# Graph network on one core: the 8-head layer's turned one-hots go to GpSimd, its rescaling to ScalarE, and each summation layer's first adjacency group gets memory of its own

## What is computed

```python
def gat_edge(x, W, a_src, a_dst, edge_W, edge_b, bias, edge_attr, src, dst):      # 8 heads
    h = (x @ W.T).reshape(n, 8, 32)
    alpha = einsum('ehd,hd->eh', h[src], a_src) + einsum('ehd,hd->eh', h[dst], a_dst)
    enc = relu(edge_attr @ edge_W.T + edge_b).reshape(-1, 8, 32)
    alpha = leaky_relu(alpha + sum(enc * h[dst], -1), 0.2)
    ex = exp(alpha - segment_max(alpha, dst)[dst])
    out = segment_sum(h[src] * (ex / segment_sum(ex, dst)[dst])[..., None], dst)
    return out + bias
def sage(x):                                   # three times, relu between
    mean = segment_sum(x[src], dst) / max(deg, 1)
    return mean @ Wl.T + bl + x @ Wr.T
def gcn(x):                                    # self-loops added, symmetric normalisation
    return relu(norm_d * segment_sum((norm_s * (x @ W))[src], dst) + b)
```

## Time and profile before

| | before |
|---|---|
| median of 3 runs | 3315.35 us (3314.17 to 3328.64) |
| profiled execution, its own time | 3314.46 us |
| its span, first to last instruction | 3312.6 us |
| TensorE busy / VectorE / ScalarE / GpSimd | 2700.5 / 1819.1 / 1223.2 / 1470.2 us |
| layer 0, from GpSimd's gathers of group 4 to those of group 51 and their period | 306.5 to 907.5 us |
| summation layers, first to last matmul | 1031.2 to 2008 us, with a node stage of some 50 us between two of them |

### The profile page before, as it was taken

How to read it: one execution, slowest core, us unless ns; L and a number is a source line. 1 busy time by engine, 2 the same in 40 slices (tenths; PEclk the granted TensorE clock), 3 DMA queues, 4 the chain that set the end, 5 groups by cost and what they waited for, 6 DMA issues and landing times.

```text
span 3312.6 us, 50756 instructions
## 1 busy us (share of the span) xinstructions
PE 2700.5 (82%) x12657; PEld 1721.4 (52%) x12658; DVE 1819.1 (55%) x4880; ACT 1223.2 (37%) x3147; POOL 1470.2 (44%) x1469
## 2 busy tenths in 40 slices
PE   6997998989989999999997997466677747766765
PEld 4774555555655545545555555344455535544543
DVE  6996999999962010000005005466666547666665
ACT  2774555555521001001001002644444454444445
POOL 5402766666613004004005001777777347777760
PEclk8998999999979999999998999777777868788785
DMA  7456877777712322322321332455545235555541
GB/s 230 130 125 171 225 214 207 206 219 209 211 21 82 100 63 77 98 70 67 101 77 62 104 98 63 131 140 136 136 136 143 77 109 136 140 141 139 138 114 40
DMA packets 310915, 421.17 MB, mean 127 GB/s; under 512 B 56707, under 2 KB 245047, under 8 KB 310367
## 3 DMA queue, kind: packets, MB, share of 16 engines
q1 hardware_dynamic: 235679, 231.06, 24.2%
q0 software_dynamic: 60544, 173.03, 19.6%
q10 hardware_dynamic: 14400, 13.93, 1.4%
HBM read 378.03 MB, written 39.84 MB: 126 GB/s over the span
## 4 chain that ended last, share of the span: by engine, by line
PE 43%; POOL 17%; issue 15%; DVE 14%; DMA 4%; ACT 4%; DVEq 2%; SPq 1%; ACTq 1%; POOLq 0%
PE ps L762 24%; POOL rows L2155 17%; PE ps L1002 3%; PE ps L633 3%; DMA rows<-table,src_idx 2%; DVE norm L1344 2%; PE ps L982 2%; PE ps L721 2%; PE ps L612 2%; ACT norm L1173 1%; PE ps L922 1%; DVE al L1350 1%; PE ps L819 1%; DVE segmax L1386 1%; PE ps L932 1%
## 5 line engine op out<-in xcount | busy, mean ns | idle before, releaser
L2155 POOL DMA_INDIRECT rows<-table,src_idx x1248 | 1251.7, 1003 | 511.6 <-issue 367.1
L762 PE MATMUL ps<-rows,rT 128*128 128x448 f16 x2800 | 765.4, 355 | 20.3 <-DMA rows<-adjacency 12.8
L762 PE MATMUL ps<-rows,spread 128*128 128x448 f16 x1400 | 497.1, 355 | 0.0
L762 PEld LDWEIGHTS ps<-rows,rT 128*128 128x128 bf16 x2800 | 275.4, 98 | 281.2 <-issue 29.2
L1556 DVE TENSOR_TENSOR rows<-ps,norm 128x896 f32<-128x896 f32 x21 | 22.9, 1092 | 636.7 <-PE ps L762 636.7
L2109 POOL CAST rT<-rows 128x1024 bf16<-128x1024 f32 (+1 forms) x28 | 30.1, 1074 | 727.6 <-ACT rows L1288 508.9
L819 PE MATMUL ps<-rows,spread 128*128 128x260 f32 x832 | 278.8, 503 | 67.6 <-DVE rows L1667 67.2
L819 PE MATMUL ps<-rows,w_roots 128*128 128x260 f32 x832 | 270.0, 490 | 37.7 <-DVE rows L1667 37.6
L819 PEld LDWEIGHTS ps<-rows,spread 128*128 128x128 f32 x832 | 207.2, 257 | 122.8 <-DVE rows L1667 71.5
L1667 DVE TENSOR_TENSOR rows<-rows,ps 128x1024 f32<-128x1024 f32 x208 | 249.0, 1197 | 30.2 <-issue 25.6
L612 PE MATMUL ps<-rT,spread 128*128 128x264 f32 x832 | 247.1, 422 | 4.1 <-DMA rT<-table 2.1
(11 more groups left out here) (270 smaller groups left out, 4302.5 us busy)
## 6 DMA issues: line engine op xcount, KB each, us to landing
rows<-adjacency SPq DMA_DIRECT2D x140, 560.0 KB, 4.0
rT<-table SPq DMA_DIRECT2D x316, 136.0 KB
spread<-in_tiles SPq DMA_DIRECT2D x104, 256.0 KB, 4.4
rows<-table,src_idx POOLq DMA_INDIRECT x1248
rT<-table ACTq DMA_DIRECT2D x100, 136.0 KB
w_table<-in_tiles SPq DMA_DIRECT2D x52, 256.0 KB
adjacency<-rT SPq DMA_DIRECT2D x4, 2800.0 KB, 13.7
adjacency<-acc SPq DMA_DIRECT2D x3, 2800.0 KB, 13.6
```

What stands on the lines that cost most here:

```text
L762: ins = mm(chunk_ps[c % 2][:, f, :], xp[k][:, t, f * P:(f + 1) * P], ring[q][:, i, :], start=t == 0 and k == 0, stop=t == ROWS - 1 and k = ...
L2155: pool.indirect_dma_start(src_rows(l, par)[:, k, :], None, tables[l][:, :], bass.IndirectOffsetOnAxis(ap=src_idx[:, g * T + k:g * T + k + ...
```

## The change

Three edits that do not depend on each other:

1. The turned one-hots of groups 4 to 51 are made by GpSimd, between the group's fourth and fifth gather, behind the wait for `h_ready` that stood there and a new wait for `high_landed`; VectorE makes those of groups 0 to 3 ahead of its loop.
2. `rescale_node` runs on ScalarE, between the fourth `encoded` and `node_sums_out`: three ACTIVATEs (two columns of `acc`, one of `den`) with a per-partition scale, and a register load for the node's number, in place of two VectorE instructions and their register load.
3. `ring[0]` moves to words 6656 to 7776 of `rows`, behind the node stage's scratch, and the other four to words 0 to 4480. The first piece of a layer waits for the node stage's first row in place of its last; the other four wait for the last row and no longer for the parts. TensorE takes the groups of chunks 0 and 1 in the order (0,0) to (0,3), (1,0) to (1,2), (0,4), (1,3), (1,4), and `USED_AT` gives the waits that follow from it. `weighed` keeps one buffer.

```diff
-        ring = [rows[:, q * PIECE:(q + 1) * PIECE].bitcast(F16).rearrange("p (h c) -> p h c", h=HQ) for q in range(NQ)]
+        ring_at = [8704 - FC * CC - 32 - PIECE] + [q * PIECE for q in range(NQ - 1)]
+        ring = [rows[:, ring_at[q]:ring_at[q] + PIECE].bitcast(F16).rearrange("p (h c) -> p h c", h=HQ) for q in range(NQ)]
...
-        weighed = [rows[:, 8704 - (b + 1) * FC * CC:8704 - b * FC * CC].rearrange("p (f n) -> p f n", f=FC) for b in range(2)]
-        more_weighed = weighed[0][:, :, 0:SPAN]
+        weighed = rows[:, 8704 - FC * CC:8704].rearrange("p (f n) -> p f n", f=FC)
+        more_weighed = weighed[:, :, 0:SPAN]
...
+        SUM_ORDER = [(0, q) for q in range(NQ - 1)] + [(1, q) for q in range(NQ - 2)] + [(0, NQ - 1), (1, NQ - 2), (1, NQ - 1)]
+        SUM_ORDER += [(c, q) for c in range(2, PIECES) for q in range(NQ)]
+        USED_AT = {of: i + 1 for i, of in enumerate(SUM_ORDER)}
+
...
-            for c in range(PIECES):
-                if c > 1:
-                    pe.wait_ge(window_added, PIECES * (l - 1) + c - 1)
-                for q in range(NQ):
+            for c, q in SUM_ORDER:
+                if c > 1 and q == 0:
+                    pe.wait_ge(window_added, PIECES * (l - 1) + c - 1)
...
+            def rescale_node(g, par):
+
+                node = act.value_load(base[0:1, bass.ds(g, 1)], min_val=0, max_val=N)
+                if isinstance(g, int) and g == 0:
+                    act.wait_ge(acc_cleared, 1)
+                act.wait_ge(resc_copied, g + 1)
+                act.wait_ge(added, g + 1)
+                for f in range(FC):
+                    col = acc[:, f, bass.ds(node, 1)]
+                    nc.scalar.activation(col, col, ACT.Copy, scale=resc_f[par][:, f:f + 1])
+                dcol = den[0:H, bass.ds(node, 1)]
+                nc.scalar.activation(dcol, dcol, ACT.Copy, scale=resc_f[par][0:H, FC:FC + 1]).then_inc(rescaled, 1)
+
...
+                rescale_node(g, j % 2)
...
-            def rescale_node(g, par):
-
-                node = V.value_load(base[0:1, bass.ds(g, 1)], min_val=0, max_val=N)
-                if isinstance(g, int) and g == 0:
-                    dve.wait_ge(acc_cleared, 1)
-                dve.wait_ge(resc_copied, g + 1)
-                dve.wait_ge(added, g + 1)
-                col = acc[:, :, bass.ds(node, 1)]
-                V.tensor_tensor(col, col, resc_f[par][:, 0:FC].unsqueeze(2), ALU.mult)
-                dcol = den[0:H, bass.ds(node, 1)]
-                V.tensor_tensor(dcol, dcol, resc_f[par][0:H, FC:FC + 1], ALU.mult).then_inc(rescaled, 1)
-
...
-                of_n, of_x = next_group(j, h, 1), next_group(j, h, 3)
+                of_n = next_group(j, h, 1)
...
-                if m is not None and not is_last(m):
-                    turned_hots(m + 1, *of_x)
...
-                rescale_node(g, j % 2)
-                if m is not None:
...
+            turned_hots(3, 3, 0)
...
-                dve.wait_ge(piece_used, NQ * (before + c + 1))
+                dve.wait_ge(piece_used, NQ * before + USED_AT[c, NQ - 1])
...
-                    V.tensor_tensor(weighed[c % 2], summed, of_nodes, ALU.mult).then_inc(window_weighed, 1)
+                    V.tensor_tensor(weighed, summed, of_nodes, ALU.mult).then_inc(window_weighed, 1)
...
-                    V.tensor_tensor(acc[:, :, of], acc[:, :, of], weighed[c % 2], ALU.add).then_inc(window_added, 1)
+                    V.tensor_tensor(acc[:, :, of], acc[:, :, of], weighed, ALU.add).then_inc(window_added, 1)
...
-                            sp.wait_ge(piece_used, NQ * PIECES * (l - 1) + at - NQ + 1)
-                        elif q < 3:
-                            sp.wait_ge(row_ready, ROWS * (l + 1))
+                            sp.wait_ge(piece_used, NQ * PIECES * (l - 1) + USED_AT[c - 1, q])
+                        elif q == 0:
+                            sp.wait_ge(row_ready, ROWS * l + 1)
...
-                            sp.wait_ge(parts_ready, NCH * l)
+                            sp.wait_ge(row_ready, ROWS * (l + 1))
...
+                            wait_alone(pool, high_landed[g % 2], 16 * (g // 2 + 1))
+                            nc.gpsimd.tensor_scalar(edge_turned[:, g % 2, :, :].rearrange("p t e -> p (t e)"), high_row[:, g % 2, :],
+                                                    rank[:, 0:1], None, ALU.is_equal).then_inc(edge_turned_ready, 1)
```

More of the change, by code:

```diff
@@ L746, in sum_pe @@
             pe.wait_ge(row_out, ROWS * (l + 1))
-            for c in range(PIECES):
-                if c > 1:
+            for c, q in SUM_ORDER:
+                if c > 1 and q == 0:
                     pe.wait_ge(window_added, PIECES * (l - 1) + c - 1)
-                for q in range(NQ):
[L752 to L764, removed]
+                if c == 0:
+                    pe.wait_ge(parts_ready, NCH * (l - 1) + 1 + -(-(HQ * (q + 1) - 1) // 4))
+                if l not in MEAN_LAYERS and q in loop_rows(c):
+                    pe.wait_ge(loops_added, loops_upto(c, q))
+                else:
+                    pe.wait_ge(piece_landed[q], 16 * (PIECES * (l - 1) + c + 1))
+                for i in range(HQ):
+                    t = HQ * q + i
+                    for f in range(FC):
+                        for k in range(PARTS):
+                            ins = mm(chunk_ps[c % 2][:, f, :], xp[k][:, t, f * P:(f + 1) * P], ring[q][:, i, :],
+                                     start=t == 0 and k == 0, stop=t == ROWS - 1 and k == PARTS - 1)
+                ins.then_inc(piece_used, 1)
             def window(w):
@@ L1989, in load_adjacency @@
                         if c > 0:
-                            sp.wait_ge(piece_used, NQ * PIECES * (l - 1) + at - NQ + 1)
-                        elif q < 3:
+                            sp.wait_ge(piece_used, NQ * PIECES * (l - 1) + USED_AT[c - 1, q])
+                        elif q == 0:
+                            sp.wait_ge(row_ready, ROWS * l + 1)
+                        else:
                             sp.wait_ge(row_ready, ROWS * (l + 1))
-                        else:
-                            sp.wait_ge(parts_ready, NCH * l)
                         sp.dma_start(ring[q], adjacency[:, q * HQ:(q + 1) * HQ, c * CC:(c + 1) * CC]).then_inc(piece_landed[q], 16)
```

## The result

The changed kernel takes 3346.16 us (median of 6 runs, 3344.89 to 3349.09) against 3314.76 us before (6 runs): ratio 1.0093, 95% interval 1.0072 to 1.0114. It is slower by about 31 us; 3284 us was forecast. The profiled execution has a span of 3345.7 us against 3312.6, 33.1 us more.

| us | before | after | difference |
|---|---|---|---|
| start to the first messages of layer 0 | 290.0 | 292.2 | +2.1 |
| first to last group's messages | 636.1 | 699.2 | +63.1 |
| from there to the first summation matmul | 105.1 | 100.2 | -4.9 |
| summation layers | 976.9 | 955.1 | -21.8 |
| 4-head layers, code untouched | 1304.5 | 1299.0 | -5.5 |

A forecast was written before the change was run, and what follows sets the result against it. Layer 0 was bound by VectorE, its 12.00 us step falling to the TensorE-ScalarE ring's 11.73: 13 us less. Summation layers gave 10.2 + 3.2 + 4.8, 18 less; together 31, so 3284 us, range 3258 to 3325.

The forecast's parts named there:

- the cast's 1.04 us: Layer 0, GpSimd: price taken for the 1024-column comparison, plus 0.1 us start, giving 11.9 us a group.
- the ring of TensorE and ScalarE: Layer 0: mutual waits of both engines, 10.98 us a step, 11.73 with the ACTIVATEs; ends last, 13 us less.
- GpSimd becomes the bound: Rival, layer 0: comparison costing as the two-input form makes groups of 13.62 us, kernel 3350 us; chance 0.10.
- the forecast's condition: Layer 0, GpSimd: comparison of about 1.05 us, so GpSimd's group stays at 11.9 us; forecast 31 us less.
- The ACTIVATEs: Layer 0, ScalarE: three instructions for rescaling add 0.75 us to the ring, bounds 0.51 and 1.17.
- the sum had 13: Layer 0: 0.27 us less per step over 48 groups, 13 us of the forecast's gain.
- over 2 us to spare: Layer 0: GpSimd's one-hots come over 2 us before TensorE's spread needs them.
- the rule: Layer 0: VectorE's two-input and GpSimd's SBUF-reading instructions exclude each other throughout; VectorE loses at most 1.04 us a step.
- the three first waits: Summation layers: TensorE's waits for the first piece in three layers, 12.8 us, shrink to 0.85 each; 10.2 us less.
- the fourth: Fourth summation layer: of TensorE's 7.5 us wait, 4.3 stay behind VectorE's self-loop adds and 3.2 go.
- the clock, of which half was taken: Summation layers' starts: shorter waits may keep TensorE's clock up; bounds 0 and 9.6 us, 4.8 taken.
- Order and late pieces: Summation layers: new group order costs nothing; later pieces stay hidden, the fifth possibly 0 to 2 us a layer.

The follow-up runs named there:

- the copy run: Changed kernel with GpSimd copying the same tiles in place of comparing them (spread features of groups 4 to 51 wrong): 3263.11 us, ratio 0.9839.
- the half run: Changed kernel with GpSimd comparing four of the eight tiles and VectorE the other four at the old place: 3292.74 us, ratio 0.9939.
- the filling matmuls: Three small unread matmuls per layer 0 step in TensorE's pauses; added to edits 2 and 3: 3270.65 us, again 3272.96; added to the changed kernel: 3348.99.

## Why the prediction was wrong

- **GpSimd's comparison: the step that failed.** The prediction took the cast's 1.04 us because the comparison has one tensor input, and set the two-input form's 2.17 us as the upper bound. It costs 2.86 us: the number of tensor inputs was the wrong likeness, and the bound wasn't one. With it GpSimd's queue, and not the ring of TensorE and ScalarE, ends last, and layer 0 is 63 us longer instead of 13 shorter. No row of the trace before showed a TENSOR_SCALAR on GpSimd. The Trainium skill ("GPSIMD Engine Reference", Engine selection) calls one-input work on GpSimd roughly line-rate; the copies' 1.04 us for 1024 columns agree, TENSOR_SCALAR's 2.77 to 2.86 us do not.
- **The rival that held.** "GpSimd becomes the bound" had the mechanism and the point from which it decides (1.77 us for what is put in), and its 3350 us lies 4 us from the result, but by luck, since errors cancel: its group of 13.62 us was 13.90 us (comparison, start and the waits that are left 3.05 us instead of 2.27, gathers longer by 0.1 instead of 0.6), and the summation layers gave 27 us instead of 18. It had a chance of 0.10, and the range stopped at 3325 us, short of it. The run with the copy shows the forecast's condition: at 1.05 us the kernel gains 53 us, more than the 31 of the forecast.
- **ScalarE and the ring.** The ACTIVATEs cost 0.56 us against 0.75 taken (0.51 to 1.17). With edits 2 and 3 alone the step is VectorE's 11.61 us, and in the copy run it goes down to 11.2: the ring's 10.98 us without them was too long by at least 0.3 us. Layer 0 is 28 us shorter there, where the sum had 13. What the prediction did not have is the clock: with edits 2 and 3 it falls in 13 of 41 steps, in the kernel before in 6, behind pauses of TensorE that both have. Such a fall makes a step of 11.6 us 0.8 to 2.6 us longer, one of the kernel before 0.3 to 0.6, and the matmuls in the pauses give 11 to 14 us of layer 0 back. Why it falls more often stays open.
- **One-hots in time.** TensorE's spread, to which the prediction gave over 2 us to spare, waits for GpSimd's one-hots in ten groups, 9.0 us in all and 2.7 us at most.
- **VectorE and the port.** Its two-input instructions are held up, as feared, but not for as long as the rule read. VectorE's timeline in the changed kernel, and GpSimd's comparison beside it:

```profile
743.75 2.20 DVE L1404 SCALAR_TENSOR_TENSOR segmax<-pens,carry_of,segmax 64x128 f32<-64x128 f32 x2
...
757.67 0.71 DVE L1404 SCALAR_TENSOR_TENSOR segmax<-pens,carry_of,segmax 64x128 f32<-64x128 f32 x2
```

```profile
744.68 2.86 POOL L2159 TENSOR_SCALAR spread<-spread,rank 128x1024 f32<-128x1024 bf16 x1
```

  The first pair ends at 745.95, 1.27 us into the comparison; the second stands free. In 27 of the 47 groups such a pair ends 1.26 to 1.28 us behind the comparison's start, though in 26 of them its second instruction had begun 0.20 to 0.64 us ahead of that start. Of the Trainium skill's rule ("SBUF — State Buffer", SBUF: two separate sides), that the loser waits for the whole instruction, the trace shows the waiting, but of 2.86 us only the first 1.27. That it costs nothing here, since GpSimd's queue sets the step anyway, is argued and not tried.
- **Summation layers.** Right in kind, too small in size: the three first waits gave 10.6 us (12.8 - 2.2; 10.2 taken), the fourth 5.4 (7.5 - 2.1; 3.2 taken, mainly since the four self-loop adds took 1.44 us instead of 3.27), and the clock, of which half was taken (4.8), gave all: the 1050 matmuls of the four layers take 198.4 us each from the first start to the last instead of 201.1, 200.1, 201.4 and 200.5, 9.3 us together before rounding. Order and late pieces cost nothing, as said.

## What to carry to other kernels

A price taken from the nearest row holds only for the same kind of instruction: before work moves to GpSimd, time the very form it will have there (a few instructions behind a layer do, run twice, since another engine can hold one of them up), because a queue that is straight code with 1.8 us of room turns an error of 1.8 us into the bound of a whole layer. Where such an unmeasured price decides, its rival needs a chance that matches, and the range must reach it. When a step is shortened, look at TensorE's granted clock step by step: here its falls behind small pauses took back half or more of what layer 0 had gained (11 of 23 us, 14 of 21), and a few spare matmuls in the pauses returned that to the layer, though not all of it to the kernel.

## What the runs showed that was not expected

- On GpSimd, TENSOR_SCALAR over 1024 columns takes 2.77 to 2.86 us when nothing holds it up, with a constant or a per-partition operand, is_equal or mult, bf16 or f32; a copy or cast 1.04, a two-input subtraction 2.34.
- VectorE's two-input instructions are held up until 1.27 us after the start of such a TENSOR_SCALAR of 2.86 us, and until 1.20 us after that of a cast of 1.05 us (the copy run). The longer of these two holds them hardly longer; the comparison of 512 columns (1.61 us, the half run) held them until 0.92 us after its start at most.
- 384 gathers with the same indices take from 384 us (the copy run) to 425 us (edits 2 and 3 with the filling matmuls). In every trace the gathers of more than 1.1 us, but for one of them, begin while VectorE's messages run.
- The granted clock falls to its lower level in single steps of layer 0, outside the loops' turns each time behind two pauses of TensorE (0.22 to 0.48 and 0.46 to 0.67 us in the kernel before and the runs with edit 3 alone and edits 2 and 3), but not behind all such pauses; with edits 2 and 3 three small matmuls a step raise its mean from 0.94 to 0.98.
